# Cross attention: keys and values as steps of their own, keys scaled on ScalarE and GpSimd

## The reference, cut to what matters

```
def attention(q, k, v):                      # scale = 1 / sqrt(16)
    scores = jnp.einsum('bqhd,bkhd->bhqk', q, k) * scale
    probs = jax.nn.softmax(scores, axis=-1)
    return jnp.einsum('bhqk,bkhd->bqhd', probs, v)
...
B, L, _ = x.shape
ctx_img = context[:, :IMG_LEN]
ctx_txt = context[:, IMG_LEN:]
q = rms_norm(linear(x, q_w, q_b), norm_q_w).reshape(B, L, NH, HD)
k = rms_norm(linear(ctx_txt, k_w, k_b), norm_k_w).reshape(B, -1, NH, HD)
v = linear(ctx_txt, v_w, v_b).reshape(B, -1, NH, HD)
k_img = rms_norm(linear(ctx_img, k_img_w, k_img_b), norm_k_img_w).reshape(B, -1, NH, HD)
v_img = linear(ctx_img, v_img_w, v_img_b).reshape(B, -1, NH, HD)
img_x = attention(q, k_img, v_img)
txt_x = attention(q, k, v)
out = (txt_x + img_x).reshape(B, L, DIM)
return linear(out, o_w, o_b)

```

## Time and profile before

| | |
|---|---|
| median of 3 runs | 2010.11 us |
| lowest, highest | 2005.04, 2010.17 us |
| the profiled execution | 2005.13 us, its span 2003.3 us |
| mean granted PE clock | 0.937 |
| PE, DVE, ACT, POOL busy | 88%, 65%, 42%, 25% |
| chain by engine | PE 64%, DVE 18%, issue 5%, DMA 5%, ACT 4%, SP's queue 2%, POOL 2% |

### The profile page before, as it was taken

One profiled execution on the slowest core, in us unless ns is written; L12 is line 12 of the kernel. 1 busy time (PEld: TensorE's weight loads), 2 busy tenths in 40 slices (PEclk: granted clock), 3 DMA queues, 4 the chain that ended last, 5 costly groups with the idle time before them and its releaser, 6 DMA issues.

```text
span 2003.3 us, 32246 instructions
## 1 busy us (share of the span) xinstructions
PE 1765.3 (88%) x12150; PEld 1102.0 (55%) x12150; DVE 1300.5 (65%) x2924; ACT 845.4 (42%) x1363; POOL 506.5 (25%) x864
## 2 busy tenths in 40 slices
PE   5998999998966979979979979998888889999977
PEld 4898888888643334434334445664454444444446
DVE  6767676766576687686678642444345687888743
ACT  2343433333331345355446732442232356666651
POOL 5443444434121020120121113441111223331200
PEclk9999999999986999999999979998897899999988
DMA  3000100110016387236055046554603057656000
GB/s 116 22 12 11 43 11 12 34 53 1 16 41 123 60 174 94 56 82 92 33 104 70 2 160 232 182 195 105 133 1 53 24 71 144 81 91 83 6 1 22
DMA packets 91396, 142.65 MB, mean 71 GB/s; under 512 B 14549, under 2 KB 59737, under 8 KB 91242
## 3 DMA queue, kind: packets, MB, share of 16 engines
q1 hardware_dynamic: 86842, 127.72, 30.4%
q10 hardware_dynamic: 2528, 7.74, 1.1%
q0 software_dynamic: 1872, 5.13, 0.7%
HBM read 109.62 MB, written 32.03 MB: 71 GB/s over the span
## 4 chain that ended last, share of the span: by engine, by line
PE 64%; DVE 18%; issue 5%; DMA 5%; ACT 4%; SPq 2%; POOL 2%; another core or an unknown queue 0%; DVEq 0%; POOLq 0%; ACTq 0%
PE bank L1181 8%; PE bank L1221 8%; PE bank L1200 7%; PE bank L1913 5%; PE bank L1523 5%; PE bank L1804 3%; PE bank L766 3%; PE bank L1806 3%; PE bank L1805 3%; PE bank L1932 2%; DVE xa_part_max L1294 2%; PE bank L2373 2%; DMA xa_qst<-xa_q_parts 2%; PE bank L2358 2%; DMA xa_k_parts<-xa_parts 2%
## 5 line engine op out<-in xcount | busy, mean ns | idle before, releaser
L1294 DVE TENSOR_REDUCE xa_part_max<-bank 128x1 f32<-128x448 f32 (+1 forms) x512 | 270.4, 568 | 66.0 <-PE bank L1181 62.0
L1255 ACT ACTIVATE xa_e<-bank 128x1024 f32<-128x1024 f32 (+1 forms) x208 | 212.4, 1021 | 133.3 <-PE bank L1200 131.5
L1255 ACT ACTIVATE ca_e<-bank 128x1024 f32<-128x1024 f32 (+2 forms) x208 | 196.3, 956 | 92.5 <-PE bank L1200 91.5
L1294 DVE TENSOR_REDUCE shared<-bank 128x1 f32<-128x400 f32 (+1 forms) x384 | 206.8, 570 | 40.5 <-PE bank L1181 36.9
L1181 PE MATMUL bank<-xa_kst,xa_qst 122*128 122x448 bf16 (+1 forms) x512 | 167.6, 365 | 45.0 <-DVE xa_part_max L1294 18.5
L1221 PE MATMUL bank<-xa_e,xa_vaug 128*17 128x256 f32 (+2 forms) x1792 | 141.0, 389 | 1.6 <-ACT xa_e L1255 0.6
L1200 PE MATMUL bank<-xa_qst,xa_kst 128*128 128x256 bf16 (+1 forms) x832 | 129.6, 279 | 4.7 <-DMA xa_qst<-xa_negT 4.7
L1221 PE MATMUL bank<-ca_e,ca_vaug 128*17 128x256 f32 (+2 forms) x1664 | 125.6, 374 | 2.0 <-ACT ca_e L1255 1.4
L1181 PEld LDWEIGHTS bank<-xa_kst,xa_qst 122*128 122x128 bf16 x512 | 45.9, 99 | 147.8 <-DVE xa_part_max L1294 86.3
L1181 PE MATMUL bank<-ca_kst,ca_qst 125*128 125x400 bf16 (+2 forms) x384 | 118.3, 341 | 7.5 <-issue 3.5
L970 POOL TENSOR_TENSOR gsa_qk<-gsa_qk,gsa_rot 128x512 f32<-128x512 f32 x64 | 81.8, 1279 | 163.0 <-DVE gsa_rot L886 163.0
(11 more groups left out here) (382 smaller groups left out, 4095.7 us busy)
## 6 DMA issues: line engine op xcount, KB each, us to landing
xa_kst<-xa_k_parts SPq DMA_DIRECT2D x96, 200.1 KB, 8.4
ca_kst<-ca_k_parts SPq DMA_DIRECT2D x96, 200.1 KB, 7.9
xa_k_parts<-xa_parts SPq DMA_DIRECT2D x8, 1200.8 KB, 6.8
ca_k_parts<-moe_ctx_parts SPq DMA_DIRECT2D x8, 1200.8 KB
moe_gu<-in_expert_gate_up SPq DMA_DIRECT2D x8, 1024.0 KB
shared<-in_ctxT_split ACTq DMA_DIRECT2D x4, 1601.0 KB, 6.6
moe_ctxT<-in_ctxT SPq DMA_DIRECT2D x8, 800.5 KB, 8.1
ca_cv<-in_ctx SPq DMA_DIRECT2D x4, 1536.0 KB
```

The lines of the kernel that those rows point to most:

```text
L1255: e.activation(self.e[m % 3][0:rows, :, first:T], banks[m % 2][0:rows].rearrange("p a (h t) -> p (a h) t", t=T)[:, :, first:T], ACT.Exp, s ...
L1294: e.tensor_reduce(top, work[:, 0:hi - lo], AX.X, ALU.max).then_inc(*reduced(t, *step))
```

## The change

- `kv` becomes two steps, `xk` (keys, and the squares on ACT) and `xv` (values), each with matmuls of 256 columns. `k_norm` follows the keys, the next `fetch` follows the values.
- In stage one only the 13 `xk` of batch 0 remain; its 13 `xv` and the fetch for batch 1 stand at positions -30 to -20 of stage two, ahead of all maxima.
- `k_scale` leaves DVE. ACT multiplies by the root (Identity with a scale per row, `k_evened`), POOL multiplies by the weight, one operation each per tile. For the mixed tile a new tensor `nk_mixed` holds both weights; SP loads it with two small DMAs after a wait for the last score product of stage one (`a_mm`). `rsqrt` signals `k_root` at its end.
- The two stores of a batch's keys signal separately (`k_stored[c]`); the load of a unit waits for the half that it reads.
- The query load of a batch's first unit is a step `load_q` of its own, two positions before its key load.
- Positions: for b = 1 `at` is `first`, for b = 2, 3 it is first - 10. Keys at + 1 to 8, queries at to at + 8, `k_scale`, `k_turn`, `k_store` at + 9 to 24, values at + 23 to 36, `load_q` at + 25, `load` at + 27.

```diff
-                        yield "kv", 0, n
-                    yield "fetch", 1
+                        yield "xk", 0, n
...
-                    q.wait_ge(k_stored, *self.k_key(b))
+                    q.wait_ge(k_stored[c], *self.k_key(b))
...
+                elif kind == "load_q":
+                    self.queries_sp(q, n)
...
-            def projections(b):
-                for n in range(NKT):
-                    yield "kv", b, n
+            def keys(b):
+                yield from (("xk", b, n) for n in range(NKT))
+                yield "k_norm", b
+
+            def values(b):
+                yield from (("xv", b, n) for n in range(NKT))
                 yield "fetch", b + 1
-                yield "k_norm", b
...
-            parts = [list(XA.flow()), *(spread(queries(b), (b - 1) * UNITS * whole_unit + 10.5, (b - 1) * UNITS * whole_unit + 21) for b in range(1, B)), [(whole_unit, ("later", 0))]]
+            first_values = spread(values(0), -30, -20)
+            parts = [first_values, list(XA.flow()), [(whole_unit, ("later", 0))]]
             for b in range(1, B):
                 first = (b - 1) * UNITS * whole_unit
-                parts += [spread(projections(b), first + 1, first + 10), spread(xa_keys(b), first + 11.5, first + 21)]
-                parts.append([(first + 27, ("load", UNITS * b))])
+                at = first if b == 1 else first - 10
+                parts += [spread(keys(b), at + 1, at + 8), spread(xa_keys(b), at + 9, at + 24), spread(queries(b), at, at + 8)]
+                parts += [spread(values(b), at + 23, at + 36), [(at + 25, ("load_q", UNITS * b)), (at + 27, ("load", UNITS * b))]]
...
+                of = slice(0, D) if kind == "xk" else slice(D, 2 * D)
...
-                        m = e.matmul(ps[r0:r1, :], xctx[:, c, k0 + r0:k0 + r1], wkv[s][:, c, :], start=(c == 0), stop=(c == DC - 1))
+                        m = e.matmul(ps[r0:r1, 0:D], xctx[:, c, k0 + r0:k0 + r1], wkv[s][:, c, of], start=(c == 0), stop=(c == DC - 1))
...
+            elif kind == "k_scale":
+                m_, = rest
+                rows = xa_tiles[m_][1]
+                q.wait_ge(k_root, n)
+                e.activation(kk[0:rows, m_, :], kk[0:rows, m_, :], ACT.Identity, scale=k_sr[0:rows, m_:m_ + 1]).then_inc(*k_evened(n, m_))
...
-            elif kind == "k_scale":
-                m_, = rest
-                q.wait_ge(dve_own)
-                q.wait_ge(xq_in, "xa")
-                for (r0, r1, s, _, _) in xa_tiles[m_][2]:
-                    m = e.scalar_tensor_tensor(kk[r0:r1, m_, :], kk[r0:r1, m_, :], k_sr[r0:r1, m_:m_ + 1], nk[s][r0:r1], ALU.mult, ALU.mult)
-                m.then_inc(*k_scaled(n, m_))
...
+            elif step[0] == "k_scale":
+                n, m_ = step[1:]
+                q.wait_ge(xq_in, "xa")
+                q.wait_ge(k_evened, n, m_)
+                k0, rows, uses, _ = xa_tiles[m_]
+                by = nk_mixed if len(uses) == 2 else nk[uses[0][2]]
+                q.e.tensor_tensor(kk[0:rows, m_, :], kk[0:rows, m_, :], by[0:rows], ALU.mult).then_inc(*k_scaled(n, m_))
...
+                q.wait_ge(a_mm, G4 * GSA_UNITS - 1)
+                for s, t in enumerate(("", "_img")):
+                    r0, r1 = xa_tiles[TXT // P][2][s][0:2]
+                    e.dma_start(nk_mixed[r0:r1], a[f"xa_norm_k{t}_w"].partition_broadcast(r1 - r0)).then_inc(*xq_in("xa", by=16))
```

More of the change, by code:

```diff
@@ L283, in boundary, with rsqrt @@
                 q.e.wait_ge(stage_done.count.sem, 5 * (n + 1))
-        def rsqrt(q, e, y, v, t):
+        def rsqrt(q, e, y, v, t, done=()):
             q.wait_ge(dve_own)
             e.tensor_scalar(y.bitcast(I32), v.bitcast(I32), -0.5, float(magic), ALU.mult, ALU.add).then_inc(*dve_own())
-            for _ in range(3):
+            for last in (False, False, True):
                 q.wait_ge(dve_own)
@@ L294, in rsqrt @@
                 q.wait_ge(dve_own)
-                e.scalar_tensor_tensor(y, t, 1.5, y, ALU.add, ALU.mult).then_inc(*dve_own())
+                e.scalar_tensor_tensor(y, t, 1.5, y, ALU.add, ALU.mult).then_inc(*(done if last and done else dve_own()))
         def rsqrt_pool(q, y, v, t):
@@ L398, in build @@
         XA_TILES = TXT // P + 1 + 2
[L399 removed]
+        XA_EARLY = ("q", "q_norm", "q_turn", "q_store", "fetch", "xk", "xv", "k_norm", "k_scale", "k_turn", "k_store", "xa_w", "xa_const", "load")
         q_mm, q_biased, q_squared, q_scaled, q_ss_taken = local("gsa", "xa_q_mm"), local("gsa", "xa_q_biased"), local("gsa", "xa_q_squared"), local("gsa", "xa_q_scaled"), local("gsa", "xa_q_ss_taken")
[L401 removed]
+        xk_mm, xv_mm, k_biased, v_biased, kt_mm = local("gsa", "xa_k_mm"), local("gsa", "xa_v_mm"), local("gsa", "xa_k_biased"), local("gsa", "xa_v_biased"), local("gsa", "xa_kt_mm")
+        k_root, k_evened = local("gsa", "xa_k_root"), local("gsa", "xa_k_evened")
         k_squared, k_scaled, k_ss_taken, k_ones = local("gsa", "xa_k_squared"), local("gsa", "xa_k_scaled"), local("gsa", "xa_k_ss_taken"), local("gsa", "xa_k_ones")
@@ L991, in build @@
         k_const, v_const = sig("att_k_const"), sig("att_v_const")
-        k_stored, q_stored = sig("att_k_stored"), sig("att_q_stored")
+        k_stored, q_stored = [sig(f"att_k_stored{c}") for c in range(DC)], sig("att_q_stored")
         mx_mm, reduced, neg_ready, neg_mm, neg_turned = sig("att_mx_mm"), sig("att_reduced"), sig("att_neg"), sig("att_neg_mm"), sig("att_neg_turned")
@@ L1128, in load_sp, with queries_sp @@
                     self.keys_sp(q, n)
+                if n not in self.queries_before:
+                    self.queries_sp(q, n)
+            def queries_sp(self, q, n):
+                b, g = divmod(n, UNITS)
+                t, e, i = self.tag, q.e, n % AHEAD
                 if n >= AHEAD:
@@ L1573, in xa_act_step @@
                     q.wait_ge(k_ss_taken, n - 1)
-                q.wait_ge(k_biased, n, m_)
+                q.wait_ge(k_biased, "xa", *step)
                 e.activation(k_sq[0:rows], kk[0:rows, m_, :], ACT.Square, accum_out=k_ss[0:rows, m_:m_ + 1]).then_inc(*k_squared(n, m_))
@@ L1579, in xa_act_step @@
                     if n:
-                        q.wait_ge(k_stored, "xa", n - 1)
+                        for stored_c in k_stored:
+                            q.wait_ge(stored_c, "xa", n - 1)
                     else:
@@ L1613, in xa_dve_step @@
                     e.scalar_tensor_tensor(qq[:, i, :], qq[:, i, :], q_sr[:, i:i + 1], nq[:], ALU.mult, ALU.mult).then_inc(*q_scaled(n * TB + i))
-            elif kind == "kv":
+            elif kind == "xk":
+                m_, = rest
+                ps = work[places[0][0]]
+                if m_ == 0:
+                    q.wait_ge(xb_in, "xa")
+                    if n:
+                        q.wait_ge(kt_mm, "k_turn", n - 1, NKT - 1)
+                q.wait_ge(xk_mm, n, m_)
+                for (r0, r1, s, _, _) in xa_tiles[m_][2]:
+                    m = e.tensor_tensor(kk[r0:r1, m_, :], ps[r0:r1, 0:D], bkv[s][r0:r1, 0:D], ALU.add)
+                m.then_inc(*k_biased("xa", *step))
+            elif kind == "xv":
                 m_, = rest
@@ L1617, in xa_dve_step @@
                 vb = XA.vaug[n % 2]
-                uses = xa_tiles[m_][2]
                 if m_ == 0:
@@ L1621, in xa_dve_step @@
                     q.wait_ge(v_const, "xa", n % 2)
-                    if n:
-                        q.wait_ge(kt_mm, "k_turn", n - 1, NKT - 1)
                     if n >= 2:
                         q.wait_ge(pv_mm, "xa", (n - 1) * UNITS - 1, "all")
-                q.wait_ge(kv_mm, n, m_)
-                for (r0, r1, s, _, _) in uses:
-                    m = e.tensor_tensor(kk[r0:r1, m_, :], ps[r0:r1, 0:D], bkv[s][r0:r1, 0:D], ALU.add)
-                m.then_inc(*k_biased(n, m_))
-                for (r0, r1, s, _, _) in uses:
-                    m = e.tensor_tensor(vb[r0:r1, m_, :, 0:HD], ps[r0:r1, D:2 * D].rearrange("p (h w) -> p h w", h=HEADS),
+                q.wait_ge(xv_mm, n, m_)
+                for (r0, r1, s, _, _) in xa_tiles[m_][2]:
+                    m = e.tensor_tensor(vb[r0:r1, m_, :, 0:HD], ps[r0:r1, 0:D].rearrange("p (h w) -> p h w", h=HEADS),
                                         bkv[s][r0:r1, D:2 * D].rearrange("p (h w) -> p h w", h=HEADS), ALU.add)
@@ L1649, in xa_dve_step @@
                     q.wait_ge(*places[1][1])
-                split_dve(q, ("xa", *step), p0, p1, r, src)
+                q.wait_ge(rounded, "xa", *step)
+                e.tensor_tensor(r, src, p0, ALU.subtract).then_inc(*rest_ready("xa", *step))
+                q.wait_ge(rest_ready, "xa", *step)
+                e.tensor_copy(p1, r).then_inc(*part1_ready("xa", *step))
         def xa_dve(q):
```

28 lines of the change are left out of this document (14 added, 14 removed).

## The result

| kernel | median, us | runs | ratio to before, 95% interval |
|---|---|---|---|
| before | 2005.26 (1998.04 to 2011.11) | 7 | |
| after | 1989.55 (1982.11 to 1996.22) | 7 | 0.9922 [0.9902, 0.9942] |

The account below looks back on a forecast made before the run. It took stage two as two stretches with different limits, PE then DVE, one behind the other. Stage two -33 and stage one's end with stage two's start -6.5 gave about -40, 2010.1 to 1970 us; range 1950 to 2001.

Parts of the forecast that it names:

- number 7: End of stage one: 12.0 us of value projection leaving is worth 11, relief of DVE 3 (ends -3 and 7).
- 1, the cut costs nothing: Projection cut into keys and values: PE's sum stays 24.1 us per batch; bounds nothing to 10% more.
- 2, the scaling: Key scaling: DVE loses 8.1 us per batch, ACT gains 13 operations of about 0.42, POOL 13 of 0.73.
- 3 and 4, the windows: Stage two: turns lose 10 us per batch, 30 in all (ends 9, 54); key and value windows PE-bound, no loss.
- The floor: Stage two evenly mixed: what PE must do takes 430 us against 505.4, so 75 at most to be had.
- the 472 forecast: Stage two's time: 430 us of PE work plus 30, 10 and 2 of losses and stalls, 33 us less.
- 5, the stall at each new batch: Batch starts in stage two: PE's 3.71 us stand for loads goes at batches 2 and 3; 0 to 3 remain.
- 6, unit 3's keys: First batch of stage two: unit 3's keys queue behind the copies and PE stalls 10 us; ends 2 and 15.
- 8, the start: After the barrier: the value projection takes 14.5 us, between 12.0 and 24.1; net +7.5 to the first maximum.
- Rival A: Queue and start take most back: unit 3 stall 15, values at 1.2 GHz, tail gains nothing; 1997 us; chance 0.24.
- Rival C: Key turn becomes a serial round over ACT, POOL, PE and DVE, 5.3 us per tile; 2075 us; chance 0.08.
- the 10 that I had feared: Shared SBUF port: 52 new POOL multiplications may each hold a DVE cast about 0.2 us, some 10 of DVE.

Follow-up runs that it names:

- columns cut: Kernel before with its 512-column projection matmuls issued as 256 columns twice, still one step and one signal: 2005.20 us, ratio 1.0012.
- wide turns in before: Kernel before with the key turns of batches 1 to 3 spread over positions 11.5 to 26.5, not 11.5 to 21: 2030.79 us, ratio 1.0128.
- cut in place: Kernel before, same order and DVE scaling, with key and value steps apart, one behind the other, and half stores signalled apart: 2003.68 us, ratio 1.0018.
- pairs and the ring of three: Changed kernel, batch 0's values in stage one right behind their keys, both on three PSUM places, copies at position 41: 1964.82 us, ratio 0.9861.

## Why the prediction was right and wrong

The step that failed is number 7, the end of stage one: "12.0 us of value projection leave it, worth 11". It is worth nothing: the tail took 1.7 us more, not 14 less, and that is 16 of the 24 us by which the sum is off. PE's 43.15 of 45 us busy were read as a bound. But the kernels with the values there, joined in the old order, have tails of 133.7 to 137.7, and those without them 134.9 to 138.5; the pair that differs in this alone has 135.4 with them and 138.5 without. The rest of that step, -3 for the relief of DVE, is nothing too: with the scaling back on DVE the tail is 134.9, with it on ACT and POOL 135.3 to 138.5.

The two rows of the whole tail say where the forecast gain went. The projection's matmuls in it fall from 26.1 us busy to 15.4, 10.7 less. PE's other work, by number the same, takes 81.1 for 76.9, 4.3 more, at a granted clock of 0.85 for 0.88, and PE is idle 41.0 for 32.8, 8.2 more: 1.7 in all. In the pair the same three are -10.5, +6.1 and +7.6. So PE's matmuls of the side work were filler between main steps that hand over from PE to ACT and DVE in a written order. After the removal PE waits longer in the same stretch for ACT, in one wait of 5.0 us where the longest had been 1.7:

```profile
PE bank L731 <- ACT gsa_qz L824: 5.0, 1, 5.0
```

and PE falls idle for a whole window, behind which the granted clock is at the lower level, 0.50, where before, as far behind the normaliser (529.5 to 537.5), it was 1.00. Two windows of after:

```profile
524.00:528.00 4.00, 0.00 (x0) 0.00 (x0) 2.39 (x13) 1.46 (x6) 1.84 (x2) 0.72 0.00 0
528.00:532.00 4.00, 3.68 (x10) 3.08 (x11) 0.32 (x1) 0.66 (x2) 0.60 (x2) 0.50 0.00 0
```

That the idle PE slowed PE's other work by the clock is argued from these rows, since no run holds the clock; what is shown is that the work's presence or absence does not shorten the tail, that its time went into idleness and slower matmuls, and that the order moves the tail.

Step by step:

- **1, the cut costs nothing:** right for the columns (1.93 us of PE per use before, 107.8 / 56, and 1.95 with columns cut, 109.0 / 56). For separate steps the group of the projection is busy 120.6 / 56 = 2.15, 3.2 us more per batch, but PE's whole busy time in stage two does not rise, so no price on PE is shown there. The tail pays 9.4 us where both halves stand there as woven steps, and that is mostly the order.
- **2, the scaling:** the prices were right within 0.1 us, but it moved nothing: stage two 482.4 with it on DVE, 480.6 and 483.0 without. Once the turns were spread, DVE had room for it: it was busy 27.25 of 30 us in the turn stretch with the scaling, and the batch was 1.0 longer.
- **3 and 4, the windows:** right in kind. PE in the turns is busy 25.45 of 30 (the forecast's 30 with its loss of 10 is 30 of 40); the value stretch PE-bound. The floor was too low: PE is busy 443.0 us in stage two when nothing stalls, against 430 worked out. Over it, without the stall, 24 us are lost, against 30 forecast. Floor +13, losses -6, the stall +4 (14 for 10) and step 5 -2 are the 9 us by which stage two lies above the 472 forecast.
- **5, the stall at each new batch:** right. No wait for query loads at units 8 and 12, and none at 4. The wide turns in before show its price: 9 to 12 us a batch if the store comes late.
- **6, unit 3's keys:** right. PE waits 9.8 there and moving the copies takes 14 us off stage two, at the long end of "10; ends 2 and 15".
- **8, the start:** right, 14.18 for 14.5 and +7.1 for +7.5 (14.5 less the idle 7.33 is 7.2, a slip of 0.3). But with 7 at nothing, the move of the values, forecast to gain 3.5 (11 - 7.5), loses 7 to 10 against a joined step in stage one (0.4% by the ratios, 3.1 + 7.3 by the parts).

The sum by measured terms: stage two -24.8 (forecast -33), start +7.1, tail +1.7, which make -16.0, the ratio's 16 us; the profiled pair's other 3.4 are the spread of other stages. Which part of the change gives stage two's 25 us is settled only in part: the scaling 1 to 2, the shift 2 to 4, the cut in place with the half stores' signals 8, and wide turns without the rest lose. No run takes the values' place behind the turns, the early query load and the half stores' signals apart. For the third batch 127 was forecast; it took 112.8, since a part of the key work in it had moved into the batches before, and the three together took 399.3 for 424.0. The first exponential came at 661.1, not near 651; that row points to step 7 at first sight, though the time ahead of the last normaliser alone wanders by 10 us.

Rival A had two of its four pieces right (the tail gains nothing, the stall is 12.5 to 14), the clock at the start spoke against it, and the batches lost 8 each rather than 13. Rival C's serial round was not seen: PE's wait for POOL's keys is 1.0 us in the second batch and 3.0 in all. By the Trainium skill ("SBUF — State Buffer", Who interferes with whom) POOL's new operations can hold DVE's casts. The trace agrees, with a small sum. In stage two the mean key cast of 128x256 rose from 297 ns to 309, 0.4 us over 36 casts. In stage one, where the turns stand closer, it rose from 317 to 417, with one cast of 0.78 us beside a POOL multiplication, 1.2 us over 12. Together that is 1.6 us, not the 10 that I had feared.

The best version of the study is the new order of stage two, the copies at position 41, and the first batch's projection in stage one at the places where the joined step stood: ratios 0.9837, 0.9840 and 0.9861 in three forms whose intervals overlap, about twice the gain of the change.

## What to carry to other kernels

A busy engine is a bound only if what keeps it busy can't move: ask of each busy stretch whether its work is on the path or fills gaps of a chain of handovers, before its removal is priced. Where side work is woven in by the number of its steps, cutting a step in two moves all the others; tie the halves first, and look for their gain after. And a DMA issue queue is part of the order: each late store or early copy is paid by what stands behind it on that queue, and the same place for the copies cost nothing in one order and 0.7% in another.

## What the runs showed of the hardware

- In stage one 4 us of idle PE, with a granted clock of 0.72, were followed by a granted clock of 0.50 in the next 4 us and 0.92 in the four after. After the barrier, behind 4.08 us of idle PE and four transposes, 56 dense fp32 matmuls took 14.18 us (14.1 to 15.6 in five kernels), at a granted clock of 0.65 in the first 4.1 us and 1.00 from 626 to 636. At the upper level's 0.216 each they would take 12.1, so it was no whole stretch at the lower level (24.1), as rival A had it.
- In the tail 112 fp32 matmuls of 256 columns were busy 26.2 us in joined steps, 27.1 in separate steps laid in pairs, and 29.1 to 30.4 in separate steps woven singly. PE's whole busy time in the tail was 102.7 us with pairs and the ring of three, as with the joined step (101.0 to 102.9), and 107.9 with single steps, where its idle time rose too, from 33 to 37.
- ACT's scaling of 128x256 by a column took 506 ns, its square of the same size 416.
- A DVE key cast of 128x256 took 296 ns alone (median) and up to 782 ns beside a POOL multiplication.
